# Rotary attention: one half of the tokens after the other, output summed in PSUM, scores 64 wide

## The reference, cut to what matters

```python
Q, K, V = (einsum('btc,ncd->btnd', x, W) + b for each of Q, K, V)   # 16 heads of 128
Q, K = rope(Q), rope(K)
scores = einsum('bqnd,bknd->bnqk', Q, K) / sqrt(128)
probs = softmax(where(causal, scores, -inf))
z = einsum('bnqk,bknd->bqnd', probs, V)
out = einsum('bnqd,ndm->bqm', z, W_O) + b_O                        # x = x + out
```

## Time and profile before

| | us |
|---|---|
| three runs | 879.61, 879.67, 888.3 (median 879.67) |
| profiled execution | 878.37 |
| its span, first to last instruction | 876.6 |
| PE, DVE, ACT, POOL busy in the span | 732.1, 632.5, 382.6, 357.3 |
| rotary attention | about 576 to 831 |

### The profile page before, as it was taken

One profiled execution on the slowest core, in us unless ns is written; L12 is line 12 of the kernel. 1 busy time (PEld: TensorE's weight loads), 2 busy tenths in 40 slices (PEclk: granted clock), 3 DMA queues, 4 the chain that ended last, 5 costly groups with the idle time before them and its releaser, 6 DMA issues. The chain is left out here.

```text
span 876.6 us, 16323 instructions
## 1 busy us (share of the span) xinstructions
PE 732.1 (84%) x5165; PEld 502.8 (57%) x5168; DVE 632.5 (72%) x1381; ACT 382.6 (44%) x1209; POOL 357.3 (41%) x292
## 2 busy tenths in 40 slices
PE   5997999687745548999996899869999999999776
PEld 4664666466612335443442666536878888888544
DVE  4446677656377854665675766659999999999777
ACT  2456656151325312212313655226454555554484
POOL 4301444227024412434353544258656565565210
PEclk9998999988958777999999999969999999999989
DMA  9452000000020002022000300011010101002101
GB/s 256 121 187 84 1 0 0 1 1 1 0 85 1 1 19 84 21 64 85 0 1 25 121 0 0 0 30 26 25 31 18 36 18 36 18 18 83 64 1 49
DMA packets 26637, 35.31 MB, mean 40 GB/s; under 512 B 10208, under 2 KB 18400, under 8 KB 25696
## 3 DMA queue, kind: packets, MB, share of 16 engines
q1 hardware_dynamic: 26592, 34.74, 12.9%
HBM read 33.68 MB, written 1.05 MB: 40 GB/s over the span
## 5 line engine op out<-in xcount | busy, mean ns | idle before, releaser
L1616 POOL TENSOR_TENSOR ra_direct<-ra_direct,ra_crossed 128x512 f32<-128x512 f32 x64 | 81.5, 1273 | 87.0 <-DVE ra_crossed L1760 87.0
L636 ACT ACTIVATE c_probs<-bank,c_neg_max 128x128 f32<-128x128 f32 x256 | 90.1, 379 | 60.2 <-DVE c_neg_max L688 60.2
L1760 DVE SCALAR_TENSOR_TENSOR ra_crossed<-bank,ra_bias,ra_sin 64x512 f32<-64x512 f32 x128 | 96.0, 750 | 1.9
L655 POOL TENSOR_TENSOR c_probs<-c_probs,c_inverse 128x512 f32<-128x512 f32 x64 | 65.3, 1040 | 71.2 <-DVE c_inverse L670 71.2
L1263 POOL TENSOR_TENSOR r_turned<-r_times_a,r_times_b 128x1024 f32<-128x1024 f32 x24 | 56.4, 2349 | 92.1 <-DVE r_times_b L1441 92.1
L601 PE MATMUL bank<-l_out_mat,c_ctx_t 128*128 128x256 f32 x256 | 61.8, 385 | 8.5 <-DVE c_ctx_t L699 8.5
L688 DVE TENSOR_REDUCE c_neg_max<-bank 128x4 f32<-128x512 f32 x64 | 41.5, 685 | 27.8 <-PE bank L65 27.8
L601 PEld LDWEIGHTS bank<-l_out_mat,c_ctx_t 128*128 128x128 f32 x256 | 46.2, 190 | 18.5 <-issue 8.4
L1719 ACT ACTIVATE ra_probs_t<-bank 128x512 f32<-128x512 f32 x32 | 19.1, 598 | 84.9 <-PE bank L1665 84.9
L636 ACT ACTIVATION_READ_ACCUMULATOR c_probs<-bank,c_neg_max 128x1 f32 x256 | 55.7, 218 | 0.0
L1724 ACT ACTIVATE ra_probs<-ra_masked,ra_neg_max 128x128 f32<-128x128 f32 x128 | 49.8, 390 | 11.1 <-DVE ra_neg_max L1779 10.7
(11 more groups left out here) (237 smaller groups left out, 2053.7 us busy)
## 6 DMA issues: line engine op xcount, KB each, us to landing
ra_raw<-l_attn_w_dram SPq DMA_DIRECT2D x16, 384.0 KB, 3.1
wq<-l_wq_dram SPq DMA_DIRECT2D x16, 256.0 KB, 3.0
wo<-l_wo_dram SPq DMA_DIRECT2D x16, 256.0 KB, 3.4
wkcq<-l_wkcq_dram SPq DMA_DIRECT2D x16, 192.0 KB, 3.1
ra_wo<-l_attn_wo_dram SPq DMA_DIRECT2D x1, 2048.0 KB, 9.7
wqr<-l_wqr_dram SPq DMA_DIRECT2D x16, 96.0 KB, 3.3
x_res<-x_dram SPq DMA_DIRECT2D x2, 512.0 KB, 4.2
wkv<-l_wkv_dram SPq DMA_DIRECT2D x16, 64.0 KB, 3.0
```

Source lines behind the costliest of these rows:

```text
L636: e = nc.scalar.activation(probs[u][:, n, :], score_bank[q][:, n - q * HP, :], ACT.Exp, bias=neg_max[u][:, n:n + 1], accum_out=total[u][:, ...
L655: nc.gpsimd.tensor_tensor(out=probs[u][:, at, :], in0=probs[u][:, at, :], in1=inverse[u][:, at].unsqueeze(2).broadcast_to([P, HP, L]), op= ...
L1616: nc.gpsimd.tensor_tensor(out=direct[e][k][:], in0=direct[e][k][:], in1=crossed[k][:], op=ALU.add).then_inc(roped, 1)
L1760: ins = nc.vector.scalar_tensor_tensor(dst[out_lo:out_lo + rows].rearrange("p t (b s) -> p (t b) s", b=2), src[lo:lo + rows], bias[v][lo:l ...
```

## The change

It is confined to `self_attention_rotary` and its mask table.

- The units go over all 16 heads on the first half of the tokens, then over all 16 on the second. The output products of a half are summed over its heads in PSUM (banks 6 and 7) and added to x once per half, at steps 18 and 34.
- The weights of a head are loaded, split by ACT and split by POOL for each unit, so 32 times instead of 16, two units ahead, with four buffers for the split parts instead of two. SP issues weights of unit n, q/k bias of unit n - 2 and v bias of unit n - 5 in one round, unrolled.
- A tile's scores are two 64 x 64 matmuls on its diagonal blocks. Even tiles write PSUM partitions 0 to 63, odd tiles 64 to 127, so the scores of four tiles fill 128 partitions x 256. Masking, exponentials and normalising work on 256 columns instead of 512, masking and the minimum become two instructions.
- Two transposes instead of four; their result is copied by two ACT instructions of 64 partitions into the diagonal blocks of `probs_t`, whose other blocks POOL has set to zero at the start. ACT waits for that memset before its first instruction. The mix is as before.

```diff
-        w_hi = [sb(f"w_hi{v}", [P, 3, CC, P], F16) for v in range(2)]
-        w_lo = [sb(f"w_lo{v}", [P, 3, CC, P], F16) for v in range(2)]
+        w_hi = [sb(f"w_hi{f}", [P, 3, CC, P], F16) for f in range(4)]
+        w_lo = [sb(f"w_lo{f}", [P, 3, CC, P], F16) for f in range(4)]
...
-        masked = [sb(f"masked{f}", [P, TH, P]) for f in range(2)]
-        probs = [sb(f"probs{f}", [P, TH, P]) for f in range(2)]
-        probs_t = sb("probs_t", [P, TH, P])
+        masked = [sb(f"masked{f}", [P, TH, S]) for f in range(2)]
+        probs = [sb(f"probs{f}", [P, TH, S]) for f in range(2)]
+        probs_t = sb("probs_t", [P, TH, 2, S])
...
-        score_bank = g.bank[3][:].rearrange("p (t n) -> p t n", t=TH)
-        turn_bank = g.bank[4][:].rearrange("p (t n) -> p t n", t=TH)
+        score_bank = g.bank[3][:, 0:TH * S].rearrange("p (t n) -> p t n", t=TH)
+        turn_bank = g.bank[4][:, 0:TH * S]
...
-                step(n, n % 4, 0)
-            with eng.Fori(1, UNITS // 4 - 1) as i:
+                step(n, n % 4, 0, 0)
+            with eng.Fori(1, H // 4) as i:
                 for f in range(4):
-                    step(4 * i + f, f, i)
+                    step(4 * i + f, f, i, 0)
+            for n in range(H, H + 4):
+                step(n, n % 4, n // 4, 1)
+            with eng.Fori(H // 4 + 1, UNITS // 4 - 1) as i:
+                for f in range(4):
+                    step(4 * i + f, f, i, 1)
             for n in range(UNITS - 4, UNITS + 3):
-                step(n, n % 4, n // 4)
+                step(n, n % 4, n // 4, 1)
...
-                if not isinstance(h, int) or h < H:
-                    sp.wait_ge(loaded[v], 16)
-                    sp.wait_ge(w_split, h - 1)
-                    sp.dma_start(raw[v][:], a["l1_attn_w"][h]).then_inc(loaded[v], 16)
-                if not isinstance(h, int) or 3 <= h <= H:
-                    sp.wait_ge(bias_loaded[w], 16)
-                    sp.wait_ge(crossing, 4 * (h - 2))
-                    sp.dma_start(bias[w][:], a["l1_attn_b"][h - 1]).then_inc(bias_loaded[w], 16)
-                if not isinstance(h, int) or h >= 4:
-                    sp.wait_ge(v_bias_loaded[v], 16)
-                    sp.wait_ge(mix_kept, 2 * (h - 3))
-                    sp.dma_start(v_bias[v][:], a["l1_attn_bv"][h - 2]).then_inc(v_bias_loaded[v], 16)
...
+            def load_bias(n):
+                v = n % 2
+                sp.wait_ge(bias_loaded[v], 16 * (n // 2))
+                sp.wait_ge(crossing, 2 * n - 2)
+                sp.dma_start(bias[v][:], a["l1_attn_b"][n % H]).then_inc(bias_loaded[v], 16)
+            def load_v_bias(n):
+                v = n % 2
+                sp.wait_ge(v_bias_loaded[v], 16 * (n // 2))
+                sp.wait_ge(mix_kept, n - 1)
+                sp.dma_start(v_bias[v][:], a["l1_attn_bv"][n % H]).then_inc(v_bias_loaded[v], 16)
+            for n in range(2, UNITS + 5):
+                if n < UNITS:
+                    sp.wait_ge(loaded[n % 2], 16 * (n // 2))
+                    sp.wait_ge(w_split, n - 1)
+                    sp.dma_start(raw[n % 2][:], a["l1_attn_w"][n % H]).then_inc(loaded[n % 2], 16)
+                if 2 <= n - 2 < UNITS:
+                    load_bias(n - 2)
+                if 2 <= n - 5 < UNITS:
+                    load_v_bias(n - 5)
...
+            nc.gpsimd.memset(probs_t[:], 0.0).then_inc(cleared, 1)
...
             split_low(0, 0)
+            split_low(1, 1)
...
-                following = next_head(n, f, i)
-                if following:
-                    split_low(*following[:2])
+                if not isinstance(n, int) or n + 2 < UNITS:
+                    split_low(n + 2, (f + 2) % 4)
...
+                if first:
+                    wait(pe, added, 2 * (n // H))
...
+                for q in range(TP):
+                    for k in range(2):
+                        hi, lo = (z[1 - e][:, 2 * q + k, :] for z in (z_hi, z_lo))
+                        factors = split_factors(hi, lo, wo_hi[:, head, :], wo_lo[:, head, :])
+                        for j, (lhs, rhs) in enumerate(factors):
+                            mm = nc.tensor.matmul(out_bank[q][:, k, :], lhs, rhs,
+                                                  start=(first and k == 0 and j == 0),
+                                                  stop=(last and j == len(factors) - 1), skip_group_check=True)
+                mm.then_inc(summed, 1)
...
-                rows = slice(e * TH, (e + 1) * TH)
+                e = f % 2
+                rows = slice(half * TH, (half + 1) * TH)
                 if project:
-                    if e == 0:
...
-                    project_to(n, v, rows, 0)
+                    pe.wait_ge(w_split, n + 1)
...
-                    wait(pe, maxed, n - 1)
+                    wait(pe, limited, n - 1)
                     for t in range(TH):
-                        mm = nc.tensor.matmul(score_bank[:, t, :], direct[1 - e][0][:, t, :],
-                                              direct[1 - e][1][:, t, :], start=True, stop=True)
+                        for b in range(2):
+                            at, k = slice(b * S, (b + 1) * S), t % 2
+                            mm = nc.tensor.matmul(score_bank[k * HD:(k + 1) * HD, t - k + b, :], direct[1 - e][0][:, t, at],
+                                                  direct[1 - e][1][:, t, at], start=True, stop=True)
                     mm.then_inc(scored, 1)
...
-                    for t in range(TH):
-                        mm = nc.tensor.transpose(turn_bank[:, t, :], probs[e][:, t, :], m.ident[:])
+                    for q in range(TP):
+                        mm = nc.tensor.transpose(turn_bank[:, q * P:(q + 1) * P],
+                                                 probs[e][:, 2 * q:2 * q + 2, :].rearrange("p t n -> p (t n)"),
+                                                 m.ident[:])
...
-                                              probs_t[:, t, :], start=True, stop=True)
+                                              probs_t[:, t, :, :].rearrange("p b s -> p (b s)"),
+                                              start=True, stop=True)
...
+            act.wait_ge(cleared, 1)
...
+                act.wait_ge(loaded[f % 2], 16 * trips)
+                wait(act, v_done, n - 3)
+                nc.scalar.activation(w_hi[f][:], raw[f % 2][:], ACT.Copy).then_inc(w_high, 1)
...
+                if not isinstance(n, int) or n + 2 < UNITS:
+                    split_high(n + 2, (f + 2) % 4, 2 * i + f // 2 + 2)
...
+                    for b in range(2):
+                        at = slice(b * HD, (b + 1) * HD)
+                        ins = nc.scalar.activation(probs_t[at, :, b, :], turn_bank[at].rearrange("p (a s) -> p a s", a=TH), ACT.Copy)
+                    ins.then_inc(turn_kept, 1)
...
+                    wait(act, summed, n - 3)
+                    act.wait_ge(v_bias_loaded[e], 16 * (2 * i + f // 2))
...
-                    for t in range(TH):
-                        if t == 0:
...
-                            dve.wait_ge(scored, n)
-                            settle(dve, n, g.passed)
-                        ins = nc.vector.tensor_tensor_reduce(
-                            out=masked[1 - e][:, t, :], in0=score_bank[:, t, :], in1=mask[:],
-                            scale=-SCALE, scalar=BIG, op0=ALU.add, op1=ALU.min,
-                            accum_out=neg_max[1 - e][:, t:t + 1])
-                    ins.then_inc(maxed, 1)
+                    wait(dve, exped, n - 2)
+                    dve.wait_ge(tables, 64)
+                    dve.wait_ge(scored, n)
+                    nc.vector.scalar_tensor_tensor(masked[1 - e][:], score_bank, -SCALE,
+                                                   mask[:, 0:S].unsqueeze(1).broadcast_to([P, TH, S]),
+                                                   ALU.mult, ALU.add).then_inc(limited, 1)
+                    dve.wait_ge(limited, n)
+                    nc.vector.tensor_reduce(neg_max[1 - e][:], masked[1 - e][:], AX.X, ALU.min).then_inc(maxed, 1)
...
-                if out:
-                    u = 1 - e
...
-                        dve.wait_ge(out_done, 2 * (n - 3) + q + 1)
-                        at = slice(u * TH + 2 * q, u * TH + 2 * q + 2)
-                        wait(dve, added, 2 * (n - 4) + q + 1)
+                    rope(n, e, 2 * i + f // 2 + 1, 1)
+                if isinstance(n, int) and n >= 3 and (n - 3) % H == H - 1:
+                    dve.wait_ge(biased, 1)
+                    dve.wait_ge(summed, n - 2)
+                    for q in range(TP):
+                        at = slice((n - 3) // H * TH + 2 * q, (n - 3) // H * TH + 2 * q + 2)
                         nc.vector.tensor_tensor(m.x[:, at, :], m.x[:, at, :], out_bank[q],
                                                 ALU.add).then_inc(added, 1)
...
+    causal = np.where(row[None, :] <= (row % S)[:, None], 0.0, 1e30).astype(np.float32)
```

(12 more changed lines are left out.)

100 lines of the change are left out of this document (30 added, 70 removed).

## The result

The change makes the kernel a little faster: median 872.84 us (868.5 to 884.13, 20 runs) against 881.6 (877.53 to 889.61, 20 runs) of the kernel before, a ratio of 0.9898 with a 95% interval of 0.9876 to 0.992. Ratios here leave out executions over 1.5% above the fastest of their kernel, such as one of these 20 and four of the ten of the start-up kernel. The forecast was 869.8 in a range of 865 to 880, a ratio of 0.9888 to the 879.67 shown then. The profiled execution took 873.15 us (span 871.3) where before took 878.37 (876.6).

What follows compares the result with a forecast made beforehand. PE was taken to bound the step at 7.52 us, the loop close behind. Terms -10.4 + 0.8 + 0.2 - 0.5 = -9.9 took the profiled 878.37 to 868.5, or 869.8 as median; range 865 to 880.

Steps and rivals of the forecast that it cites:

- What bounds it, what DVE's relief is worth alone: Rotary attention step: PE sets it at 7.52 us, the two-step loop is close behind; taking work from DVE alone gains nothing.
- Rival 4: DVE relief does nothing, as PE and the loop were the limits: forecast without score and transpose gains, 880; no separate chance.
- Transposes -0.22: Transposes on PE, per step: four become two, which takes 0.22 us off PE's step.
- Scores 0.70: Score matmuls on PE: 64 wide passes on two column halves run side by side, 0.70 us a step instead of 0.89.
- rival 1: Score matmuls keep strict program order at the column halves: scores 0.98, PE's step 7.39, time 876.5; chance 0.16.
- The doubt that the prediction named: Score matmuls: halves alternate in the cross attention row relied on, but here two matmuls go to each half in turn; unsized.
- The loop takes over at 7.15: Dependent loop from mix over z_hi, z_lo, ropes and POOL's add to scores: 14.29 us per two steps, above PE's 7.11.
- 28 x 0.37 = -10.4: Steady steps of the rotary attention: 0.37 us saved in each of 28 units, the first four being start-up; -10.4 us.
- rival 3: v bias lands late for z_hi on SP's queue: at the longest landing the step is 8.15, time 897.8; chance 0.07.
- Start +0.8: Stage's start: memset before ACT's first weight and extra POOL subtractions leave the fifth unit 0.8 us late.
- Half way +0.2: Between the token halves: the two residual adds stand once in DVE's order, mostly under the z_hi wait; +0.2 us.
- End -0.5: Stage's end: narrower scores, exponentials, normalising, transposes shorten the last chain, adds wait for the whole last output; -0.5 us.

Runs made afterwards that it cites:

- start-up kernel: Changed kernel with memset and three low parts of the output weights moved to DVE, bias add moved to units 16 to 19; median 873.42 us, ratio to before 0.9873.
- order and sum only: Changed kernel with scores, mask, normalising and transposes 128 wide as before the change; ratio to the kernel before 1.0036.
- second run: The changed kernel itself, unedited, run again on the same chip with a second profile; ratio to the kernel before 0.9902.
- alternating kernel: Changed kernel with its score matmuls alternating strictly between the two column halves; ratio to the kernel before 0.9888.

## Why the prediction was right, and where not

- *What bounds it, what DVE's relief is worth alone.* Right: 7.51 with order and sum only. Rival 4's picture stands for that part.
- *Transposes -0.22.* Right, from both sides: 7.17 to 7.39 when doubled.
- *Scores 0.70.* They took 0.75 of PE's step, nearest to the forecast's case. The overlap is there as the cross attention's rows told; the 0.05 too much is the price of two matmuls per half in a row, as the alternating kernel shows (0.62 instead of 0.66). The doubt that the prediction named was the right one. Strict order (rival 1) is out for this order of halves: its 0.98 was not seen. The rule of the Trainium skill that was quoted against this part ("TensorE: Matmul & The Clock Gate", part 3) has matmuls start and end in program order. The rows do not name each pass's half, but two starts 0.006 apart among eight passes of one half speak against that wording for fp32 passes on two halves; and the cost drawn from it, overlap at boundaries alone, fails here, as twice as many passes had begun when the halves alternate.
- *The loop takes over at 7.15.* This step failed, though the number nearly fits. PE sets 7.17; the loop has 0.20 to spare over two steps, so it is at 7.07. In the sum for two steps (14.29 forecast, 14.14 measured) the largest miss is the way from the mix to z_hi, which starts 0.20 after the q projection (711.15, 711.35) where 0.34 was carried over from before, so that z_lo is 0.92 behind instead of 1.06. In other steps it is 0.28, and in before it was 0.20 too near the end, where its steps are unrolled; why it varies is open. From z_lo to the end of POOL's add are 7.39 instead of 7.46, of which the masked scores are 0.06 (0.80 from the mask's start at 707.87 to the next rope's at 708.67). From the scores to the end of the mix PE needs 5.78 instead of 5.72.
- *28 x 0.37 = -10.4.* Measured over 27 steps: C fell by 7.73, made of 26 x 0.34 and 0.16 for the last, shorter one, together 9.0, less 1.3 for late steps. The forecast's 0.37 took the step before as 7.52 (7.51) and the one after as 7.15 (7.17). The late v bias (rival 3) happened, in two steps and not in all: after most requests it landed in time.
- *Start +0.8.* At the same clock it was +1.3 (A +0.56, B +0.72), as POOL is full until 615 us; before the fifth unit's scores PE also waited 1.7 us for the last low part of the output weights. In the second run, with a shorter low stretch, A and B together were only 0.7 above before. The start-up kernel takes 2.2 of A and B out again.
- *Half way +0.2.* Too much: 0.03 more than the others for the step in which the adds stand (7.20). *End -0.5:* D fell by 0.34 in this profile and rose by 0.51 in the second, where the low stretch in it was 10.2 us instead of 6.8. In the three profiles with the narrow scores and before's 6.8 us it fell by 0.34 to 0.56: about right. *Feed-forward weights 0:* no wait for them was found.
- *Sum -9.9.* The yardstick gives -6.8 and -7.2, the medians -8.8. What the yardstick leaves out is the code ahead, which is the same in both kernels and whose time scatters by more than that; between the two lie 0.002 of the ratio, as much as its interval to either side. The mechanism at PE was right. Of the 3.1 us between -9.9 and -6.8 the late steps are 1.3, the start 0.5, and the step (0.34 for 0.37, in 26 steps for 28) 1.4. That the ratio (0.9898) came within 0.001 of the forecast's (0.9888) is partly luck: by the yardstick the stage gave 6.8 to 7.2 us of the 9.9.

## What to carry to other kernels

Narrow matmuls that fill only half of the array's columns pay if neighbours in program order go to different halves; alternate them strictly. Relief of an engine that is not the bound is worth nothing by itself, but may be what a second change needs: 0 with wide scores, 0.16 us a step with narrow ones. When work is moved to an idle engine at a stage's start, look at what its neighbour reads at that time. Compare the kernels from a common point behind the untouched code, and look at the granted clock on both sides before a difference of 1 us is put down to the edit.

## What had not been expected of the hardware

- A two-input fp32 subtraction of 128x1024 takes 1.21 to 1.23 us on DVE and 2.13 on POOL alone, and 2.68 to 3.14 and 2.73 to 3.11 when both run such work. Each then ends 1.08 to 1.09 (DVE) or 1.98 to 1.99 us (POOL) after the other engine's instruction: one goes after the other, and nothing is gained. The ropes, whose input is in PSUM, take their 0.75 beside POOL's adds. The Trainium skill ("GPSIMD Engine Reference", 1. Specifications) says that the two engines share the SBUF interface and that DVE instructions with two SBUF inputs contend; the runs agree.
- A pass of 64 columns in fp32 follows another on the same half after 0.058 us, and one on the other half after 0.007 to 0.014, so that a block of 16 takes 0.90, 0.66 or 0.62 us by the order alone. Four 128 wide matmuls (8 passes) took 0.89, so with four of one half in a row the narrow form gained nothing.
- Untouched stages took up to 12 us more in one profile than in another, with the granted clock of the whole between 0.917 and 0.940.
- The low stretch (0.50) at the stage's start lasted 13.7 us in one profile of the change and 10.2 in the other; the seven profiles with the change's start show an A of 21.10 with the longer one and of 20.38 or 20.62 with the shorter.
